# A mixture of experts in a vision tower: the dense expert goes, all eight are sorted, and the first rows are gathered by a product

## The reference, cut to what matters

```python
x = x + _attention(_layernorm(x, ln1_g, ln1_b), Wqkv, Wproj)
x = x + _moe(_layernorm(x, ln2_g, ln2_b), Wrouter, W1, W2)

def _moe(x, Wrouter, W1, W2):                 # 576 tokens, DIM 192, FF 768, 8 experts
    logits = xf @ Wrouter
    topk_w, topk_idx = jax.lax.top_k(logits, K)        # K = 2
    topk_w = jax.nn.softmax(topk_w)
    we = zeros((N, E)).at[arange(N)[:, None], topk_idx].add(topk_w)
    for each expert:                                   # a scan
        h = gelu(xf @ W1e)                             # 576 x 768
        acc = acc + we_e[:, None] * (h @ W2e)
```

## Time and profile before

| | |
|---|---|
| median of 3 runs | 407.72 us (403.25 to 407.98) |
| profiled execution | 402.83 us, span 401.0 us |
| granted TensorE clock in it | 0.97 of full |
| PE busy, DVE busy, ACT busy, POOL busy | 90%, 69%, 59%, 32% of the span |
| the experts' block | from 296.4 us to the end |

### The profile page before, as it was taken

How to read it: one execution, slowest core, us unless ns; L and a number is a source line. 1 busy time by engine, 2 the same in 40 slices (tenths; PEclk the granted TensorE clock), 3 DMA queues, 4 the chain that set the end, 5 groups by cost and what they waited for, 6 DMA issues and landing times. The chain is left out here.

```text
span 401.0 us, 8441 instructions
## 1 busy us (share of the span) xinstructions
PE 361.2 (90%) x2724; PEld 287.7 (72%) x2724; DVE 275.4 (69%) x654; ACT 237.1 (59%) x641; POOL 128.1 (32%) x161
## 2 busy tenths in 40 slices
PE   8999799999998789999888999787959889999994
PEld 5336466666668678887776777665859679999983
DVE  1668799999972673446886438788647649765656
ACT  3566878988850406676455366666437177866640
POOL 2101413333300431425564216555366002121100
PEclk9999899999999999999999999999879989999998
DMA  8374434345404600699000065200235546300031
GB/s 164 54 228 95 101 102 106 95 126 125 116 14 118 251 1 0 213 287 260 25 2 2 2 254 189 82 3 2 81 83 186 174 163 203 120 12 21 3 101 45
DMA packets 23424, 42.19 MB, mean 105 GB/s; under 512 B 4772, under 2 KB 17092, under 8 KB 23256
## 3 DMA queue, kind: packets, MB, share of 16 engines
q1 hardware_dynamic: 21848, 39.46, 34.7%
q0 software_dynamic: 1024, 1.97, 1.4%
q10 hardware_dynamic: 512, 0.24, 0.2%
HBM read 38.29 MB, written 9.27 MB: 119 GB/s over the span
## 5 line engine op out<-in xcount | busy, mean ns | idle before, releaser
L557 PE MATMUL ps<-weights,hT 120*96 120x288 f32 x320 | 81.6, 411 | 0.9 <-DVE weights L395 0.9
L557 PEld LDWEIGHTS ps<-weights,hT 120*96 120x96 f32 x320 | 51.7, 166 | 24.8 <-DVE weights L395 1.5
L395 DVE SCALAR_TENSOR_TENSOR weights<-dist_y,hat_x 120x576 f32<-120x576 f32 x80 | 60.4, 795 | 1.7 <-PE ps L557 1.2
L1133 ACT ACTIVATE a_probs<-ps,a_minus_peak 108x108 f32<-108x108 f32 (+1 forms) x144 | 47.2, 340 | 11.0 <-DVE a_minus_peak L1196 11.0
L1293 POOL TENSOR_TENSOR a_probs_n<-a_probs,a_inv_sums 108x324 f32<-108x324 f32 (+1 forms) x48 | 39.1, 815 | 42.0 <-DVE a_inv_sums L1203 41.0
L314 POOL TENSOR_TENSOR h_step<-h_act 96x600 f32<-96x600 f32 x14 | 26.6, 1899 | 69.7 <-DVE weights L395 69.7
L464 ACT ACTIVATE dist_y<-pos,row_shift 120x576 f32<-120x576 f32 x64 | 46.8, 769 | 1.4 <-DVE weights L395 1.0
L1775 PE MATMUL ps<-slot_w,hT_hi 128*128 x90 | 27.8, 371 | 4.2 <-DVE hT_lo L1986 3.9
L1904 POOL DMA_INDIRECT yk_dram<-x,dest x12 | 12.6, 1047 | 59.5 <-DVE x L1997 59.5
L1133 ACT ACTIVATION_READ_ACCUMULATOR a_probs<-ps,a_minus_peak 108x1 f32 (+1 forms) x144 | 29.5, 205 | 0.0
L1196 DVE TENSOR_REDUCE a_minus_peak<-ps 108x3 f32<-108x324 f32 (+1 forms) x48 | 21.4, 447 | 8.8 <-PE ps L1025 8.7
(11 more groups left out here) (222 smaller groups left out, 873.5 us busy)
## 6 DMA issues: line engine op xcount, KB each, us to landing
pos<-pos_dram SPq DMA_DIRECT2D x16, 540.0 KB, 4.5
raw<-in_w SPq DMA_DIRECT2D x8, 768.0 KB, 4.5
xg_dram<-in_pad SPq DMA_DIRECT2D x1, 5304.0 KB, 22.7
raw<-in_w SPq DMA_DIRECT2D x7, 576.0 KB
patches<-in_patches SPq DMA_DIRECT2D x6, 216.0 KB, 5.7
hid<-xg_dram SPq DMA_DIRECT2D x9, 136.0 KB, 2.4
dcn_w<-in_dcn_w SPq DMA_DIRECT2D x1, 1152.0 KB, 11.2
yk_dram<-in_pad SPq DMA_DIRECT2D x1, 864.0 KB, 27.8
```

Of the source, the lines that this page charges most:

```text
L395: nc.vector.scalar_tensor_tensor(weights[:, t, :], dist_y[:, t, :], 1.0, hat_x[:, s, :], ALU.min, ALU.mult).then_inc(weights_ready, 1)
L557: ins = nc.tensor.matmul(ps[0:C1, 2 * (b % 2) + a, 0:HALF], hT[:, b % 2, t, :], weights[:, t, a * HALF:(a + 1) * HALF], start=(t == 0), st ...
L1133: nc.scalar.activation(probs[0:n, u % 3, j, 0:n], ps[0:n, u % 4, j * n:(j + 1) * n], ACT.Exp, bias=minus_peak[0:n, u % 4, j:j + 1], accum_ ...
```

## The change

Three things change. Expert 0 is sorted like the others, so the dense matmuls, gelus and adds go, and there are 16 tiles in place of 15 (`TILES_E`). The rows of the first four tiles (`FIRST_E`) no longer come back from DRAM: DVE writes for each of them a matrix of ones and zeros (`find`, 128 x 640) that says which token stands in which row, and PE multiplies the tokens' x by it (`tile_finds_x`, 20 matmuls), which gives x already transposed. Their gates and destinations still come from DRAM by four small loads (`load_meta`, `meta_first`). And `split_w1_rest` of experts 4 to 7 moves from DVE to POOL. In the places where the dense matmuls stood, the PE gets `fill`: matmuls with zeros, 4 and 8 at the end of the attention, 6 and 12 in the experts' block. Beside that `raw2` has three buffers, both kinds of slots seven, expert 3 is split in the attention's turns, the last `rest` sum moves from POOL to DVE, ACT and DVE split the tokens' x for the gathering (`rows_high`, `rows_low`), and x's low part is one instruction of DVE where it was two.

```diff
-TILES_E = (2 * NTOK + (EXPERTS - 1) * 127) // 128
+TILES_E = (2 * NTOK + EXPERTS * 127) // 128
+FIRST_E = 4
-TURN_ACT = {0: [(1, 5), (2, 4)], 1: [(1, 6)], 2: [(2, 5)], 3: [(1, 7)], 4: [(2, 6)], 5: [(2, 7)]}
-TURN_DVE = {1: [(1, 5), (2, 4)], 2: [(1, 6)], 3: [(2, 5)], 4: [(1, 7)], 5: [(2, 6)], 6: [(2, 7)]}
+TURN_ACT = {1: [(2, 3)], 2: [(1, 5), (2, 4)], 3: [(1, 6), (2, 5)], 4: [(2, 6)], 5: [(1, 7)], 6: [(2, 7)]}
+TURN_DVE = {0: [(2, 1)], 1: [(2, 2)], 2: [(1, 4), (2, 3)], 3: [(1, 5)], 4: [(2, 4), (1, 6)], 5: [(2, 5)], 6: [(1, 7), (2, 6)], 7: [(2, 7)]}
+TURN_POOL = {0: 5, 2: 6, 4: 7}
...
+def fill(nc, P, times):
+    for _ in range(times):
+        nc.tensor.matmul(P["ps"][:, 4, 0:256], P["zeros"][:, 0:128], P["zeros"][:, :], start=True, stop=True)
...
                     scatter_rows(nc, P, following, 0, 0)
-                    scatter_rows(nc, P, following, 0, 1)
-                    base(XT - 1)
...
+                next_w2(3)
+                sp.wait_ge(map_ready, 2)
+                sp.wait_ge(W["scattered"], 16 * 2 * XT)
+                load_meta(0)
+                load_rows(FIRST_E)
+                for i in range(1, FIRST_E):
+                    load_meta(i)
+                for i in range(FIRST_E + 1, FIRST_E + SET):
+                    load_rows(i)
...
+                def tile_finds_x(i):
+                    pe.wait_ge(W["rows_lo_done"], 3)
+                    pe.wait_ge(found, i + 1)
+                    if i >= 1:
+                        pe.wait_ge(tile_xT_copied, DC * i)
+                    for c in range(DC):
+                        at = slice(c * 128, (c + 1) * 128)
+                        for t, (t0, n) in enumerate(XTILES):
+                            for a, half in enumerate((rows_hi, rows_lo)):
+                                ins = nc.tensor.matmul(ps[:, 7, at], half[0:n, t, at], found_at[i][0:n, t, :], start=(t == 0 and a == 0), stop=(t == XT - 1 and a == 1))
+                    ins.then_inc(tile_xT_ready, 1)
...
                 for t in range(AHEAD, XT):
                     route_logits(nc, P, W, t)
-                for f in range(3, FT):
-                    up_ahead(nc, pe, P, W, f)
+                fill(nc, P, 6)
                 route_counts(nc, pe, P, W, 1)
                 totals()
-                for f in range(FT):
-                    up_late(f)
-                for t in range(XT):
-                    down(t)
-                tile_transposes_x(0)
-                tile_transposes_x(1)
+                fill(nc, P, 12)
+                tile_finds_x(0)
+                tile_finds_x(1)
                 for i in range(TILES_E):
                     tile_ups(i)
-                    if i + 2 < TILES_E:
+                    if i + 2 < FIRST_E:
+                        tile_finds_x(i + 2)
+                    elif i + 2 < TILES_E:
                         tile_transposes_x(i + 2)
...
+                pool.wait_ge(W["scattered"], 16 * 2 * XT)
+                split_w1_rest(nc.gpsimd, W, 4)
+                pool.wait_ge(W["w1_rest_done"], 5)
                 for i in range(SCATTERED):
                     scatter_y(i)
+                    if i in TURN_POOL:
+                        pool.wait_ge(y_scattered[i % 2], 16 * (i // 2 + 1))
+                        split_w1_rest(nc.gpsimd, W, TURN_POOL[i])
+                        pool.wait_ge(W["w1_rest_done"], TURN_POOL[i] + 1)
...
-                w2_low(1)
+                rows_low(nc, dve, W, 0)
                 best_two(nc, dve, P, W, 1)
                 choices(nc, dve, P, W, 1)
-                w2_low(2)
+                rows_low(nc, dve, W, 1)
+                tile_map()
+                find(0)
+                find(1)
+                places(nc, dve, P, W, 1)
+                slots()
                 gates(nc, dve, P, W, 1)
-                places(nc, dve, P, W, 1)
-                tile_map()
-                w1_low(3)
-                add(0)
...
```

More of the change, by code:

```diff
@@ new lines, in stage_experts @@
+        apart = sb("apart", [128, XT, EXPERTS])
+        apart_of = gelu_out[:, 1, 0:FIRST_E * XT * EXPERTS].rearrange("p (i t e) -> p i t e", i=FIRST_E, t=XT)
+        place_of = sb("place_of", [128, FIRST_E, XT])
+        place_in = sb("place_in", [128, FIRST_E, XT])
+        rows_hi, rows_lo = rows_halves(W)
+        found_at = [W["slot_lo1"][:, slot, 0:XT * 128].rearrange("p (t j) -> p t j", t=XT) for slot in (4, 5, 6, 5)]
+        first_meta = sb("first_meta", [128, FIRST_E, 2 * EXPERTS])
@@ L1938, in tile_map @@
-                    route.done(nc.vector.tensor_scalar(around[:, :], tile_expert[:, :], float(SLOTS_2 + 1), -float(SLOTS_2), ALU.is_ge, ALU.mult))
-                    nc.vector.tensor_scalar(slot1_at[:, :], tile_expert[:, :], -1.0, None, ALU.add).then_inc(map_ready, 1)
+                    route.done(nc.vector.tensor_tensor(shifted[:, :, :], of_tile[:, :, :], shift[:, :].unsqueeze(1).to_broadcast((128, TILES_E, EXPERTS)), ALU.mult))
+                    route.done(nc.vector.tensor_tensor(apart_of, of_tile[:, 0:FIRST_E, :].unsqueeze(2).to_broadcast((128, FIRST_E, XT, EXPERTS)), apart[:, :, :].unsqueeze(1).to_broadcast((128, FIRST_E, XT, EXPERTS)), ALU.mult))
@@ new lines, in tile_map, with find @@
+                    route.wait()
+                    route.done(nc.vector.tensor_tensor(place_in[:, :, :], place_of[:, :, :], row_first[:, :].unsqueeze(2).to_broadcast((128, FIRST_E, XT)), ALU.subtract))
+                    route.wait()
+                def find(i):
+                    if i == FIRST_E - 1:
+                        dve.wait_ge(tile_xT_ready, 2)
+                    nc.vector.tensor_tensor(found_at[i], place_no.unsqueeze(1).to_broadcast((128, XT, 128)), place_in[:, i, :].unsqueeze(2).to_broadcast((128, XT, 128)), ALU.is_equal).then_inc(found, 1)
@@ L1944, in tile_map, with slots @@
+                def slots():
+                    route.done(nc.vector.reduce_sum(tile_expert[:, :], begun[:, :, 0:EXPERTS], axis=AX.X))
                     nc.vector.tensor_tensor(row_at[:, :], row_f[:, :], tile_row, ALU.add).then_inc(map_ready, 1)
+                    route.wait()
+                    route.done(nc.vector.tensor_scalar(around[:, :], tile_expert[:, :], float(SLOTS_W + 1), -float(SLOTS_W), ALU.is_ge, ALU.mult))
+                    route.wait()
+                    nc.vector.scalar_tensor_tensor(slot_at[:, :], tile_expert[:, :], -1.0, around[:, :], ALU.add, ALU.add).then_inc(map_ready, 1)
```

344 lines of the change are left out of this document (157 added, 187 removed).

## The result

The changed kernel takes 414.3 us (median of 4 runs, 408.15 to 415.24) beside 407.3 for the kernel before: a ratio of 1.024 (95% interval 1.015 to 1.033). A second set of runs gave 1.036 (1.020 to 1.051). The prediction was 407.4 us in 400.5 to 412.5, with 0.06 for "slower by over 2%". It is slower, by 6 us or more; whether by over 2%, the first set leaves open. The profiled execution took 413.85 us, span 411.7, for 402.83 and 401.0 before.

A forecast was written before the change was run, and what follows sets the result against it. The prediction took the block's first part as waiting on DRAM and its middle as bound by PE. Its terms, -8.4 + 1.8 + 4.33 + 2.4 - 0.4 = -0.3 us, led to 407.4 us, range 400.5 to 412.5.

The forecast's parts named there:

- Item 1: Start of the experts' block: POOL's and PE's last work ends sooner, so the block starts 1.0 us earlier.
- Item 2: Up to the downs of tile 1: they start at 325.4 instead of 333.81, waiting for metadata, -8.4 us.
- the clock stays down: Rival, chance 0.16: PE at half clock through the third gathering at the block's start, +5.3 us, giving 412.7.
- Item 3: Tiles 2 and 3: ACT's W1 and W2 splits delay each tile's downs, +1.8 us, between 0 and 2.6.
- Item 4: The sixteenth tile: one more tile's work, all on PE, +4.33 us.
- Items 5 and 6: Tile 7 waits for expert 7's `rest` on POOL, +2.4 us; two later periods lose waits on splits, -0.4 us.
- the port: Rival, chance 0.12: POOL's last three `rest` and DVE's splits block each other, three times on the path, +5.4 us, giving 412.8.

The follow-up runs named there:

- e12: The changed kernel run again unedited, for a second profile; ratio 1.036 to the kernel before.
- e11: Changed kernel with 40 and 10 fills around the first gathering, W1's `rest` back on DVE, splits dealt one to a tile, SP's loads reordered; ratio 1.000 to the kernel before.
- e7: Changed kernel with 40 and 10 fills, last gates, places and metadata loads earlier, `rest` on DVE, splits dealt one to a tile; 400.0 us, ratio 0.9945 to the kernel before.
- e9: Changed kernel with splits dealt one to a tile, SP's loads reordered and `rest` on DVE, its own fills and gate order kept; ratio 1.007 to the kernel before.
- e4: Changed kernel with `split_w1_rest` of experts 4 to 7 moved back from POOL to DVE; ratio 1.014 to the kernel before.
- e2: Changed kernel without the fills of 6 and 12 at the start of the experts' block; ratio 1.020 to the kernel before.
- e1: Changed kernel with the second row of fills 40 instead of 12; ratio 1.026 to the kernel before.
- e5: Changed kernel with 40 fills instead of 12 ahead of the first gathering and 10 more between first and second; ratio 1.014 to the kernel before.
- e6: Changed kernel with 40 and 10 fills, plus last gates and places ahead of the second `find` and metadata loads ahead of the row loads; ratio 1.009 to the kernel before.

## Why the prediction was wrong, step by step

*Item 1* (block starts 1.0 us sooner): not testable at that size, the start moves by up to 9 us between profiles. From the last weight load to the block it was 15.7 us before, 15.3 changed: 0.4 where 1.0 was forecast. But it was 13.8 in e12, the same program, so this doesn't settle it either.

*Item 2* (-8.4 to the downs of tile 1) is the step that failed, in one assumption: that the gatherings run at the full clock, 2.2 us each, and PE is ready 3.0 us ahead of the metadata. With the clock held, the downs of tile 1 start 30.3 us after the block's start (e11); the step said 30.0 (325.4 less 295.45). Part of that is luck. The metadata came when it said (27.8 us after the start, for 27.7), though SP's loads go out 1.1 us apart and not 0.86. But PE is not early: the 3.0 us to spare were not there, since its own path takes 30.1 us (e7, where the metadata comes sooner) for the 27.0 forecast (322.4 less 295.45). A gathering takes 2.6 us of PE's chain even at full clock, for 2.2, and the first starts 9.4 us after the block's start, for 8.65. In the changed kernel gatherings took 4.66 and 5.07, and the ups 3.50 for 1.77. e9 against e11 prices the clock at 5.2 us at tile 1; the rival *the clock stays down* said +5.3. Its price came out right by two errors that cancel: it counted three slow gatherings where two were slow, and took off the 3.0 us of spare time that did not exist. Its chance of 0.16 was too low: the text itself named the wait of "1.5 us or more" for `find`, with the earlier trace rows showing the clock lost in front of the first ups. It should have been the forecast.

*Item 3* (+1.8): 3.4 came. Its own mechanism, ACT's splits, was there but smaller than said: waits of 1.01 and 0.32 in tiles 2 and 3, for 1.25 each. (Its terms, 3 x 4.33 + 2.5, give 15.5 and +2.0, not 15.3 and +1.8.) The larger wait, 1.56 in tile 4, it left out: the port, and in its place, as e4 shows, DVE's doubled turns. e9 shows that the dealing, with at most one split of ACT to a tile, takes the stalls away.

*Item 4* (+4.33): 4.1.

*Items 5 and 6* (+2.4 and -0.4): +1.7 together, for +2.0, and e4 takes off 1.9. The port rival was right in kind and happened on the path once (1.5 us), not three times; e4 shows that DVE's own work would have filled that place.

Sum: the forecast had +0.7 from the block's start on, the trace has +7.6; 5.7 of the 6.9 between them are item 2 and 1.6 item 3, and the others give 0.4 back. The range ended at 412.5, since it left out the clock and item 3 at their upper ends together. And two rivals that both lengthen the block were taken as alternatives, where they added up.

## What to carry to other kernels

Before you give TensorE a stretch of new matmuls behind a wait, price them at both clocks and let the slow price decide if a pause like those here (1 to 3 us) stands in front or in between, since such a pause lowered the clock in some places here and not in others; filler work has to run up to the very instruction it protects, since filler that ends early bought nothing here (e2), and filler that covered one of two pauses made the block longer (e1). A gain at the head of a pipeline stays only if the queues behind it (here the weight splits on ACT and DVE and the loads they wait for) are dealt and ordered for the earlier start: e5 gained 5.1 us at tile 1 and kept nothing, e11 kept 4.4 of 5.2. Compare kernels from a landmark that repeats, not from the start of the program.

## What the runs showed of the hardware

- A pause of TensorE of 0.99 us, after a gathering at full clock, was followed by the lower clock (1.2 GHz) for 17 us, though PE was busy 15.00 of 15.00 us in the window of e1 above. After the pause of 2.95 us in the changed kernel it stayed low for 13.5 us, with a second pause of 0.99 us in it. After the waits ahead of tile 7 in e1, e5, e6 and e12 it came back within 3 to 4 us, and after waits of 1.0 to 1.9 us in the changed kernel's tiles 2, 4 and 7 it never fell. The Trainium skill's "TensorE: Matmul & The Clock Gate", section "A second HAM failure mode: psum-queue depth-cycling", says of another kernel that short, frequent idles between groups of matmuls made the clock swing; the trace agrees that such idles can be enough, but here it was a single pause of 0.99 us, with the copy between two gatherings through one PSUM bank.
- Twenty matmuls of 128x128 on 128 columns in fp32r take 2.77 to 2.86 us at full clock, 4.87 to 5.07 at the lower one.
- One W1 load behind five others landed after 8.12 us (e5).
